# Signs of binarized weights on GpSimd and in their own stage, loads reordered, one norm moved into the last unit, queries and keys projected ahead of values

## The reference

```python
x = x + tanh(g_xattn[0]) * xattn0(layernorm(x), ctx)         # 16 heads of 16, softmax
x = x + tanh(g_ffn[0])   * binary_ffn(layernorm(x))          # w -> w + (mean|w| * sign(w) - w)
x = x + tanh(g_xattn[1]) * xattn1(layernorm(x), ctx, mask)
x = x + tanh(g_ffn[1])   * fp8_gemm(layernorm(x))
x = x + tanh(g_xattn[2]) * align(layernorm(x), ctx)
x = x + tanh(g_ffn[2])   * channel_mix(layernorm(x))
x = x + tanh(g_xattn[3]) * xattn3(layernorm(x), ctx)
y = layernorm(x)
for i in range(6):        # 16 heads of 64, windows of 64 tokens with the window before
    y = attn_layer(shift_tokens(y), Wqkv[i], q_scale[i], k_scale[i], Wo[i]) + y   # l2norm, rotary, softmax
    y = ffn_layer(shift_tokens(y), ln_g[i], ln_b[i], W1[i], b1[i], W2[i], b2[i]) + y
x = x + tanh(g_ffn[3]) * y
```

## Time and profile before

| | before |
|---|---|
| median of 3 runs | 5487.08 us (5486.08 to 5490.51) |
| the profiled execution's own time | 5484.13 us |
| its span, first to last instruction | 5482.8 us |
| busy: TensorE, VectorE, ScalarE, GpSimd | 4912.0, 3421.7, 3134.3, 2343.1 us |
| mean granted TensorE clock | 0.965 |

### The profile page before, as it was taken

One profiled execution on the slowest core, in us unless ns is written; L12 is line 12 of the kernel. 1 busy time (PEld: TensorE's weight loads), 2 busy tenths in 40 slices (PEclk: granted clock), 3 DMA queues, 4 the chain that ended last, 5 costly groups with the idle time before them and its releaser, 6 DMA issues.

```text
span 5482.8 us, 92490 instructions
## 1 busy us (share of the span) xinstructions
PE 4912.0 (90%) x35528; PEld 3015.9 (55%) x35528; DVE 3421.7 (62%) x6534; ACT 3134.3 (57%) x6626; POOL 2343.1 (43%) x2266
## 2 busy tenths in 40 slices
PE   4888889989898888887999999999999999999997
PEld 1223323334343333226777777777777777777775
DVE  3665556575756566766766666666666666666663
ACT  2555455434343434555767666676767667676672
POOL 1111011111110101107767666666767666666762
PEclk7999999999999989998999999999999999999998
DMA  4232222131212221311000000000000000000000
GB/s 102 49 56 53 44 52 58 38 73 37 58 36 41 44 41 40 64 26 51 15 17 19 19 23 19 25 17 21 21 19 24 17 23 17 24 18 17 24 9 31
DMA packets 125063, 188.96 MB, mean 34 GB/s; under 512 B 18800, under 2 KB 67568, under 8 KB 124400
## 3 DMA queue, kind: packets, MB, share of 16 engines
q1 hardware_dynamic: 124624, 183.06, 14.9%
HBM read 150.09 MB, written 32.51 MB: 33 GB/s over the span
## 4 chain that ended last, share of the span: by engine, by line
PE 65%; DVE 18%; ACT 9%; issue 6%; POOL 2%; DMA 1%; SPq 0%; DVEq 0%; ACTq 0%; POOLq 0%
PE psum L1212 15%; PE psum L1260 8%; PE psum L455 5%; PE psum L1261 4%; PE psum L420 4%; PE psum L441 3%; DVE maxes L641 3%; ACT probs L820 2%; PE psum L402 2%; PE psum L1269 2%; PE psum L1302 2%; PE psum L1293 2%; PE psum L1284 2%; PE psum L464 2%; DVE sums L674 2%
## 5 line engine op out<-in xcount | busy, mean ns | idle before, releaser
L820 ACT ACTIVATE probs<-psum 128x1024 f32<-128x1024 f32 x768 | 770.0, 1020 | 608.3 <-PE psum L441 337.8
L641 DVE TENSOR_REDUCE maxes<-psum 128x1 f32<-128x1024 f32 x512 | 615.1, 1211 | 307.9 <-PE psum L420 304.4
L1403 DVE TENSOR_TENSOR lwork<-psum,rotary 128x512 f32<-128x512 f32 x384 | 265.0, 690 | 781.8 <-ACT lwork L1505 745.4
L1530 ACT ACTIVATE lprobs<-psum,small_stats,stats 128x128 f32<-128x128 f32 x1536 | 579.9, 460 | 196.3 <-DVE small_stats L1421 195.4
L1590 POOL TENSOR_TENSOR stats<-stats,minus_half 128x8 f32<-128x8 f32 x384 | 640.4, 1668 | 32.0
L1586 POOL TENSOR_TENSOR lwork<-lwork 128x512 f32<-128x512 f32 x384 | 492.9, 1284 | 328.8 <-DVE lwork L1405 328.8
L420 PE MATMUL psum<-stack 96*128 96x512 bf16 x1536 | 482.6, 397 | 133.7 <-ACT probs L820 102.1
L441 PE MATMUL psum<-stack 98*128 98x512 bf16 x1536 | 517.6, 393 | 69.7 <-DVE maxes L641 37.5
L932 POOL TENSOR_TENSOR attn<-attn,sums 128x512 f32<-128x512 f32 x48 | 60.8, 1267 | 1160.6 <-DVE sums L674 1160.6
L1505 ACT ACTIVATE lwork<-psum 128x512 f32<-128x512 f32 x384 | 231.4, 602 | 383.9 <-PE psum L1261 383.3
L638 DVE CUSTOM_DVE_ANT_0 psum<-psum,mask_by_query 128x1024 f32<-128x1024 f32 x256 | 313.9, 1227 | 186.8 <-PE psum L420 185.1
(11 more groups left out here) (230 smaller groups left out, 12346.7 us busy)
## 6 DMA issues: line engine op xcount, KB each, us to landing
stack<-k_parts SPq DMA_DIRECT2D x288, 128.0 KB
staged<-in_quads SPq DMA_DIRECT2D x144, 256.0 KB, 2.7
k_parts<-parts SPq DMA_DIRECT2D x48, 384.0 KB, 2.9
stack<-q_parts SPq DMA_DIRECT2D x288, 64.0 KB
staged<-in_w SPq DMA_DIRECT2D x54, 256.0 KB, 2.7
ctx<-in_ctxT SPq DMA_DIRECT2D x24, 512.0 KB, 4.6
q_parts<-parts SPq DMA_DIRECT2D x24, 384.0 KB, 2.3
arena<-in_ctxT SPq DMA_DIRECT2D x8, 512.0 KB, 4.3
```

What stands on the lines that cost most here:

```text
L641: ins = vector.tensor_reduce(to, pair(("M", u)), AX.XY, ALU.max)
L820: scalar.activation(probs[:, i % 6, :, :], pair(("E", u)), ACT.Exp).then_inc(S_["E_act"], 1)
L1530: ins = scalar.activation(pr[:, h, :], scores(u)[:, h % 2, h // 2, :], ACT.Exp, bias=st[:, 4 + h:5 + h], scale=y[:, h:h + 1])
```

## The change

- Weights: `bz` becomes `bA` (ScalarE: absolute values of an eighth of `w_ff` into `magnitudes`, the not yet used half of the arena), `bP` (TensorE: one mean for every output column from its eighths in one go; ScalarE copies it out) and `bS` (ScalarE: signs of an eighth; GpSimd: the three elementwise steps). They stand at turns 0 to 47 of unit 0.
- Loads: x comes first for batch 0 alone; batches 1 to 3 (`xi`), the output weights, `w_ff`, the bias and the fp8 weights come after the loads of stack 0, which stand in the list right behind the third product. `JOBS` has the two key products of a feature half behind its query product, and `st` of a group waits for the three products of its half alone. VectorE's wait for the bias moves to `m1`.
- The norm of batch 2 stands at turns 728 to 734 + LAG, in unit 11, instead of behind the last unit.
- Part two: the six matmuls of queries and keys come first, with a semaphore of their own (`qk_pe`), for which VectorE now waits; then the six of the values. ScalarE copies the values first, waits for VectorE's products and squares then; the sum of squares waits for the square, which is also what leaves the queries' bank. TensorE waits for the values' bank only before their matmuls.

```diff
+JOBS = [(kind, m, n) for m in range(C) for kind, n in (("q", 0), ("k", 0), ("k", 1))]
+MEANS = [(0, 2), (1, 3), (4, 5, 6, 7)]
...
+    signs = [[("bA", 0), ("bA", 2)], [("bA", 1), ("bA", 3)], [("bP", 0)], [("bA", 4), ("bA", 5)], [("bP", 1)], [("bA", 6), ("bA", 7)], [], [("bP", 2)]]
+    signs += [x for i in (0, 2, 1, 3, 4, 5, 6, 7) for x in ([], [("bS", i)])]
+    turns.insert(next(i for i, (t, x) in enumerate(turns) if ("pk", (0, 0, 2)) in x) + 1, (-3, [("st", GROUPS[0]), ("xi", 0), ("wl", "L0_o"), ("wl", "L0_ff")]))
...
-    turns += [(64 * 12 + LAG + 20, x) for b in (2, 3) for x in last_norm(b)]
+    turns += [(64 * 11 + LAG + 24 + j, x) for j, x in enumerate(last_norm(2))]
+    turns += [(64 * 12 + LAG + 20, x) for x in last_norm(3)]
...
+                elif stage == "bP":
+                    PE.wait_ge(S_["bA_act"], max(at_("bA", i) for i in MEANS[u]))
+                    left(one, ("bP", u), PE)
+                    n = D if u == 2 else S
+                    chunks = [magnitudes[:, i, j * n:(j + 1) * n] for i in MEANS[u] for j in range(S // n)]
+                    for i, part in enumerate(chunks):
+                        ins = tensor.matmul(bank(("bP", u))[:, 0:n], ones_mean[:, :], part, start=i == 0, stop=i == len(chunks) - 1)
...
+                elif stage == "bA":
                     A.wait_ge(S_["ff_in"], 16)
+                    scalar.activation(magnitudes[:, u, :], ff_slot(u), ACT.Abs).then_inc(S_["bA_act"], 1)
...
+                elif stage == "bS":
+                    G.wait_ge(S_["bP_act"], at_("bP", k))
+                    G.wait_ge(S_["bS_act"], at_("bS", u))
+                    pool_step(gpsimd.tensor_tensor(sg, sg, mean, ALU.mult))
+                    pool_step.join()
+                    pool_step(gpsimd.tensor_tensor(sg, sg, w, ALU.subtract))
+                    pool_step.join()
+                    gpsimd.tensor_tensor(w, w, sg, ALU.add).then_inc(S_["bS_pool"], 1)
...
-            sync.dma_start(bias_b[:, :], a["L1f_bias"]).then_inc(S_["bias_in"], 16)
-            sync.dma_start(w_ffb[:, :, :], a["L1f_w"]).then_inc(S_["k8_in"], 16)
...
-                    for j in range(6):
+                    for j in range(3 * (g // 2), 3 * (g // 2) + 3):
...
-        LEAVES = {"qkv": ("qkv_dve", "qkv_act"), "tr": ("tr_act",), "pt": ("pt_act",), "pv": ("pv_dve",), "ot": ("ot_dve",), "wo": ("add_dve", "add_dve"),
+        LEAVES = {"qkv": ("sq_act", "qkv_act"), "tr": ("tr_act",), "pt": ("pt_act",), "pv": ("pv_dve",), "ot": ("ot_dve",), "wo": ("add_dve", "add_dve"),
...
+                    for i, (to, lo, hi, sem) in enumerate(((qk, 0, 512, "qk_pe"), (vp[:, 0:256], 512, COLS, "qkv_pe"))):
+                        left(one, ("qkv", u, i), PE)
+                        for c in range(C):
+                            for n, (x_, w_) in enumerate(((xs_hi, wh), (xs_hi, wl), (xs_lo, wh))):
+                                ins = tensor.matmul(to, x_[:, c, b % 2, tok(tt)], w_[:, c * COLS + lo:c * COLS + hi],
+                                                    start=c == 0 and n == 0, stop=c == C - 1 and n == 2)
+                        ins.then_inc(S_[sem], 1)
...
-                    V.wait_ge(S_["sq_act"], at_("qkv", u))
+                    V.wait_ge(S_["qk_pe"], at_("qkv", u))
...
-                    scalar.activation(buf("sq", u), bank(("qkv", u, 0)), ACT.Square).then_inc(S_["sq_act"], 1)
...
+                    A.wait_ge(S_["qkv_dve"], at_("qkv", u))
+                    left(work_at, ("sq", u), A)
+                    scalar.activation(buf("sq", u), bank(("qkv", u, 0)), ACT.Square).then_inc(S_["sq_act"], 1)
...
-            sync.dma_start(X[:, c, :, PAD:ROW], a["xT"][c * P:(c + 1) * P, :, :]).then_inc(x_in, 16)
+            sync.dma_start(X[:, c, 0, PAD:ROW], a["xT"][c * P:(c + 1) * P, 0, :]).then_inc(x_in, 16)
```

More of the change, by code:

```diff
@@ L292, in first_part @@
         yq = arena[:, 7680:8192].bitcast(BF16)
+        magnitudes = hidden
+        ff_slot = lambda i: w_ff[:, i * S:(i + 1) * S]
+        sign_at = lambda i: {0: 2, 2: 2, 1: 3, 3: 3, 4: 5, 5: 6, 6: 5, 7: 6}[i]
         w1 = w_ff[:, 0:FF0 * D].rearrange("p (c n) -> p c n", c=C)
@@ L465, in tensor_program @@
                     ins.then_inc(S_["wo_pe"], 1)
-                elif stage == "bz":
-                    half, n0, n, nc_ = CHUNKS[u]
-                    left(one, ("bz", u), PE)
-                    for c in range(nc_):
-                        PE.wait_ge(S_["bz_abs"], BZ[u] + c + 1)
-                        tensor.matmul(bank(("bz", u))[:, 0:n], ones_mean[:, :], buf(("bz", u, 0))[:, 0:n],
-                                      start=c == 0, stop=c == nc_ - 1).then_inc(S_["bz_pe"], 1)
+                elif stage == "bP":
[5 more added lines that the diff above has]
+                        ins = tensor.matmul(bank(("bP", u))[:, 0:n], ones_mean[:, :], part, start=i == 0, stop=i == len(chunks) - 1)
+                    ins.then_inc(S_["bP_pe"], 1)
                 elif stage == "f0a":
                     b, i = u
-                    PE.wait_ge(S_["bz_end"], len(CHUNKS))
+                    PE.wait_ge(S_["bS_pool"], 8)
                     PE.wait_ge(S_["ln3_dve"], at_("ln3", ("f0", b)))
@@ L899, in gpsimd_program @@
         def gpsimd_program():
+            pool_step = at.pool_step
             G.wait_ge(S_["half_set"], 1)
@@ L914, in gpsimd_program @@
                     gpsimd.tensor_tensor(sq[0], sq[0], sq[1], ALU.add).then_inc(S_["ln1_pool"], 1)
+                elif stage == "bS":
+                    k = next(i for i, x in enumerate(MEANS) if u in x)
+                    n = D if k == 2 else S
+                    wide = lambda x: x.rearrange("p (j n) -> p j n", n=n)
+                    sg, w, mean = wide(magnitudes[:, sign_at(u), :]), wide(ff_slot(u)), bc(magnitudes[:, MEANS[k][0], 0:n], 1, S // n)
+                    G.wait_ge(S_["bP_act"], at_("bP", k))
[5 more added lines that the diff above has]
+                    gpsimd.tensor_tensor(w, w, sg, ALU.add).then_inc(S_["bS_pool"], 1)
                 elif stage == "ln2":
@@ L959, in sync_program @@
                         sync.dma_start(l2_att[:, :], a[u]).then_inc(S_["l2att_in"], 16)
+                elif stage == "xi":
+                    for b in range(1, B):
+                        for c in range(C):
+                            sync.dma_start(X[:, c, b, PAD:ROW], a["xT"][c * P:(c + 1) * P, b, :]).then_inc(S_["xs_in"], 16)
                 elif stage == "cx":
@@ L1019, in sync_program @@
                         sync.dma_start(at.x_kept[c * P:(c + 1) * P, b, :], tokens(b, c)).then_inc(kept[b], 16)
-        BZ = [sum(CHUNKS[i][3] for i in range(n)) for n in range(len(CHUNKS))]
         tensor_program()
```

83 lines of the change are left out of this document (26 added, 57 removed).

## The result

| | before | after |
|---|---|---|
| median | 5488.8 us (5486.08 to 5493.14, 4 runs) | 5414.15 us (5403.35 to 5415.6, 4 runs) |
| profiled execution's own time, span | 5484.13, 5482.8 us | 5413.98, 5412.7 us |
| mean granted TensorE clock | 0.965 | 0.964 |

The ratio is 0.9859, 95% interval 0.9842 to 0.9876: the change takes 1.4% away, about 75 us of the 107 that the prediction's terms add up to. The span fell by 70.1 us. I split it at three places that both programs have: the first exponent matmuls, the first copy of values in part two, and the end.

The account below looks back on a forecast made before the run. Engines waiting for each other bound the start; in part two TensorE is busy 2804 of 2960 us, leaving 156. Terms -57-48+1-2.5 = -106.5 from the 5487.1 median gave 5381, range 5339 to 5433.

Parts of the forecast that it names:

- my own case: Whole kernel: the summed terms hold, giving 5381 us, with its own range 5350 to 5415 and chance 0.58.
- The wait for att_lo, -43: Part two: TensorE's 43.4 us of projection waits for VectorE's L1435 all go; bounds -25 to -43.
- The wait at the values' product, -21: Part two, L1302: its 33.1 us of waits go, but about 41 of 55 keep 0.3 us; bounds -10 to -33.
- I take +3: Part two, late-VectorE turns: the queries' bank comes free a square later, partly offset by VectorE's earlier queue; bounds -10 to +14.
- the +14 that I had for the square: Part two: 22 waits of L1260 for the products grow 0.65 us each, before credit for VectorE's earlier queue.
- ScalarE, +6: Part two: turns where ScalarE's table loads and exponents hold the square cost 6 us; bounds 0 to +15.
- (a): Part two, queries and keys multiplied before values: all its terms together give -57 us, range -85 to -20.
- part two's waits only move: Rival: part two's waits shift to the square, exponents or ScalarE, so it gains only 5 us: 5433; chance 0.2.
- Loads that stick out, 0: Part two: weight loads behind consecutive 256-column matmuls add 0 us, of a possible 0 to 15.
- (b): Start: bias wait, loads and weight stages changed, first exponent matmuls at 85 instead of 133.05: -48 us, bounds -43 to -56.
- GpSimd, +1: Unit 0: GpSimd's elementwise steps on the weights delay its projection steps by 1 us; bounds 0 to +8.
- (c): End of part one: moving one norm saves 6.8 us there and costs 4.3 in unit 11: -2.5, bounds -6.8 to +1.

Follow-up runs that it names:

- sq_first: The changed kernel, but ScalarE squares queries and keys first, right after their six matmuls, and VectorE's products wait for the square: 5361.11 us, ratio 0.9772 to the kernel before.
- p2_old: The changed kernel with part two's projection code on TensorE, ScalarE and VectorE as before: 5440.26 us, ratio 0.9919 to the kernel before.
- bz_old: The changed kernel with the old weight stage `bz` and part two as before, keeping the new loads and product order: 5486.28 us, ratio 0.9987 to the kernel before.
- loads_old: The changed kernel with old product order, large loads ahead of stack 0, and stack 0 behind all six products: 5412.06 us, ratio 0.9862 to the kernel before.
- norm2_back: The changed kernel with the norm of batch 2 behind the last unit again: 5413.43 us, ratio 0.9861 to the kernel before.
- ff_early: The changed kernel with the `w_ff` load right behind the context, ahead of the first product stores: 5400.5 us, ratio 0.9831 to the kernel before.

## Why the prediction was right, and where its sizes were off

The sign and the main mechanisms were right, and 5414 lies in the range of 5339 to 5433; the forecast of 5381 was 33 us too low, and the upper bound of my own case, 5415, was only just met. Step by step:

- **The wait for att_lo, -43: right.** The row is gone.
- **The wait at the values' product, -21: right.** 33.1 fell to 8.6, that is -24.5, with 0.26 us in 33 turns where I had put 0.3 in 41.
- **The step that failed: "I take +3" for the turns in which VectorE is late.** Measured are +34.6 (22.8 to 57.4), in 49 turns instead of 22. In the 26 turns behind a norm step the wait grew by 14.9 us (26.1 to 41.0), 0.57 each; that is nearly the +14 that I had for the square, and the credit for VectorE's earlier queue, which took it down to 3, didn't show. In the turn shown above VectorE had stood 2.12 us for ScalarE's `xn_hi`, so an earlier queue of its own could not help it. The other 23 turns, 16.5 us, had no term at all. In 22 of them the wait is 0.69 or 0.70 us: the cast ahead of the products takes 1.55 us instead of 0.43, and the square comes behind that. sq_first shows both parts: the wait falls by 20.8 us in the 26 turns, and by 16.5 in the 23, where the casts are short again.
- **ScalarE, +6: too small.** Waits of the scores for ScalarE went from 7.8 us in 15 turns to 20.4 in 49, and 5.5 once for the keys at the start.
- **What no term had: the clock.** The changed kernel has 11 waits of 1.8 to 2.2 us at L1266, and behind 10 of them TensorE fell to its lower level for a few microseconds. In the six other kernels with this part two it did so behind 6 to 10 of the 11, so the wait alone doesn't decide. The longest of the kernel before was 1.58.
- Together (a) came to -27.5 in the profiled executions instead of -57 (the ratios of after and p2_old give -33). That is inside its bounds of -85 to -20, about halfway to my rival "part two's waits only move", which had -5 for it and gave the whole 5433.
- **Loads that stick out, 0: right.** 256-column matmuls behind one another start every 0.120 us (median), and the twelve of a tile take 2.07 us from the first start to the last in both kernels.
- **(b), the start, -48: right,** -50.6, with 45 to 51 by the eight kernels that have this start. Every step on the way was near: norm at 9.4 (8.9), first stack issue at 36.5 (37.2), tile 0 at 47.8 (49.4), `w_ff` at 57.6 (59 to 60), first mean at 58.8 (61), E0 at 82.5 (85). But the text left open what was worth what; by bz_old the weight stages are worth 43 us at E0 by themselves, and by loads_old the order of loads next to nothing beside them.
- **GpSimd, +1 (bounds 0 to 8): off.** Unit 0 lost 8.0 us in this execution and 3.4 to 14.2 in the others, going with a granted clock of 0.95 to 0.83 over the stretch; thin GpSimd steps took nothing away that can be told from that, and the signs are worth 1 to 2 us of waits. Why the clock fell in one execution and not in another stays open.
- **(c), the norm, -2.5: right.** By norm2_back -3.8, as +4.3 in unit 11 and -8.1 behind it, where I had +4.3 and -6.8.

In the profiled executions the parts add up so: -50.6 at the start, +8.0 in unit 0, +2.7 in units 1 to 10 (2068 us before; between 2065 and 2079 in the other kernels), +5.3 in unit 11 and -8.1 behind it, -27.5 in part two: -70.2, the 70.1 of the span but for rounding.

## What to carry to other kernels

When a release moves from one engine's instruction to another's behind it, price it in every turn in which the engine ahead is late, and give no credit for an earlier queue before seeing what that engine stands for (here it was ScalarE's `xn_hi`). Then look for steps of two engines that the new order brings together: 23 of the 49 waits had to do with a cast that grew from 0.43 to 1.55 us when GpSimd's step started at the same moment or a few ns ahead. And put the reader that can start first ahead of the one that is often late, not behind it: with ScalarE's square in front, a late VectorE holds the bank for its own products alone, and the same change is worth 2.3% instead of 1.4%.

Two edits at the start that pull at the same load are to be tried apart: an early stack and a late weight cancelled each other, and the DMA time in between stood idle until the weights' load was moved there (from 10 to 20 us the DMA engines' share is 0.05 after, 0.60 in ff_early).

## What the runs showed of the hardware

The same instructions took 103 to 114 us from E0 to the fourth shift step, with a granted clock of 0.95 to 0.83 over the stretch, from one execution to the next. The four executions of norm2_back show what that does to the whole: with mean granted clocks of 0.961, 0.963, 0.966 and 0.966 they took 5429.77, 5419.16, 5407.69 and 5403.01 us. That hides anything in part one that is worth less; part two's length repeats within 0.4% (2942.4 to 2952.6 us in seven kernels with the changed one's part two). So an edit of a few microseconds has to be read from a stretch of the trace and not from the total.

One VectorE instruction, the cast of 128x512 at L1484, takes 0.43 us or 1.55 us, by a few nanoseconds: in 23 of the 24 long ones of the changed kernel GpSimd's L1610 starts 1 to 4 ns ahead of it and in one 1 ns behind; in sq_first it starts at least 5 ns behind, and no cast is long. The mechanism is not shown by a run of its own.

The Trainium skill (TensorE: Matmul & The Clock Gate, "What's actually happening") says that the number of matmuls at the lower clock at a kernel's start differs from run to run of one kernel, and that this ramp costs under 1% of a typical kernel. The trace agrees as to the size, and shows such differences far behind the start too, with the 0.95 to 0.83 above and 10.8 us between the shortest and the longest such stretch, 0.2% of 5414; only, that is more than the norm, the signs and the order of loads are worth together.
